# Two mixers, one image pair at a time: the next pair's statistics, logits and softmax among row 7's steps, and row 0's keys and queries in two parts

## Chip, cores and metric

The kernel runs on one core of a Trainium2 chip, in one launch. The metric is device time in microseconds; before the change it is 3754.8 us, the median of three runs (3750.45 to 3756.43). Less is better.

## The reference, cut to what matters

```python
# x: (16, 56, 56, 192) float32
x = x + outlook(_gn(x))     # first mixer
x = x + windows(_gn(x))     # second mixer
# _gn: 32 groups of 6 channels, mean and variance over all positions of an image
# outlook: a = softmax over 9 of (x @ W_attn + b_attn) per head (6 heads); v = x @ W_v + b_v
#          y = sum over the 3x3 neighbourhood of a * v;  y @ W_proj + b_proj
# windows: roll by (-3, -3), 7x7 windows, qkv = xw @ qkv_weight.T + qkv_bias, 12 heads of 16
#          softmax(q*k/4 + relative bias + shift mask) @ v, @ proj_weight.T + proj_bias, roll back
```

## The kernel before, in words

Two images are worked on together (a pair; 192 channels of two images fill three tiles of 128 partitions: tile 0, tile 1 with half of each image, tile 2). A hardware loop runs over the eight pairs. The activation `xa` of a pair stays in SBUF. Within one pass:

1. **Outlook.** Seven chunks of 8 rows each. TensorE repeats attention weights over channels (`reps`, L480), VectorE multiplies them with shifted values (L1339), GpSimd and accumulating DMAs add the nine products, TensorE projects. The logits and softmax of a chunk are worked out during the chunk before it. For chunk 0 that is done at the end of the pass before.
2. **Statistics of the second norm.** VectorE's `bn_stats` and `bn_aggr`, small vector steps (`moments`, L1386), one-column and two-column matmuls that average over groups (`group_moments`, L568), a square root on ScalarE, then `xw`, the normalized row 0.
3. **Windows.** Eight rows of eight windows, each row 392 tokens. Row w+1's queries, keys and values are made while row w's attention runs. A row has eight steps; a step handles two windows and half of the heads: scores (L671) on TensorE, bias and maximum (L1436, L1439, L1446) on VectorE, subtraction (L1667) on GpSimd, exponential (L1055) on ScalarE, sum and reciprocal (L1453, L1456) on VectorE, product (L1674) on GpSimd, transpose of the probabilities (`turn_probs`, L700) on TensorE, copy to SBUF (L1065) on ScalarE, and for every second step the product with the values (`attend`, L717). Scores run three steps ahead of `turn_probs`. The values go from PSUM to `vs` (L1049) and from there by four DMAs per half row, on SP's queue (L290), to `vbd`, which `attend` reads.
4. **Row 7 and the end of the pass.** In row 7 no further row has to be prepared. There stand the last loads of the next pair (`turn_next`), the output transposes of rows 5 and 6 (`turn_out`, L735), the group means and variances of the next pair (`group_means`, `group_variances`, steps 4 and 5), its square root (an `ACT_TABLE_LOAD` for Sqrt in step 5, one for Exp in step 6) and its normalized chunk 0 (`normalize`, step 6). After row 7 come, one behind another: the logits of chunk 0 (L380 to L384), the wide part of its values, the output projection of row 7, `turn_logits`, the softmax on VectorE and ScalarE, its split into three bfloat16 parts (`soft_split`, `back`), row 7's output transposes, and `turn_weights` (L426), on which the next pass's first `reps` wait.

The order on each engine is written out by hand; each engine executes its own list in order and waits on counting semaphores. So a wait holds back all that stands behind it on that engine. PSUM has eight banks; R0, R1 (4, 5), TURN_BANK (6) and Y_BANK (7) are used in turn, banks 0 to 3 hold scores. The steps that the change touches are in `ring`, `ring_last`, `beside` and `window_row`, each of which exists once per engine.

Of the kernel before, what the change touches and what calls it, by code (L numbers as in the profile page):

```python
# [9 lines left out]
ALU = mybir.AluOpType  # L10
ACT = mybir.ActivationFunctionType
# [62 lines left out]
QUERIES = SLOT + N  # L74
ONE = 16
# [9 lines left out]
def mixer(nc, x, wa, ba, wv, bv, wp, bp, wqkv, bqkv, wo, bo, table, sel_in, gmat_in, mask_in, out):  # L85
    ctx = ExitStack()
    with ctx:
# [90 lines left out]
        e_agg = sem("e_agg"); e_kept = sem("e_kept"); g_two = sem("g_two"); xw_zero = sem("xw_zero")  # L178
# [17 lines left out]
        counted = [e_agg, e_kept, g_two, xw_zero, *x_in, x_turned, x_kept, x_stat, g_agg, g_table, g_mean, g_dev, g_sq, g_var, g_std, g_rstd,  # L196
# [130 lines left out]
        def _(pe):  # L327
# [31 lines left out]
            def group_variances(g, bank):  # L359
                pe.wait_ge(g_sq, ONE + g + 1)  # L360
# [99 lines left out]
            middle(5, wot, 0, 2, bias[:, 4, :].unsqueeze(2), 1).then_inc(bout_mm, 1)  # L460
            pe.wait_ge(w_cast, 1)

            def first_weights(G):
                turn_weights(G, 0, FIRST_BANK)
                pe.wait_ge(a_kept, ONE + 2 * G + 1)
                turn_weights(G, 1, FIRST_BANK)

            with pe.Fori(0, NP) as i:
# [42 lines left out]
                def prepare(c, n):  # L511

                    G = G0 + c
                    if n < 2:
                        logits_part(G + 1, n, SOFT_BANK)
# [76 lines left out]
                first_weights(G0)  # L592
                pe.wait_ge(v_kept, ONE + T * (G0 + 1))
                pe.wait_ge(ot_kept, ONE + NT * NW * i)
# [18 lines left out]
                def first_keys(banks):  # L613

                    a, b, src = P[:, banks[0], 0:RT], P[:, banks[1], 0:RT], xw[:, 0, :, :]
# [4 lines left out]
                    mm(a, wt[:, 0, C:C + 128], src[:, 0], start=False, stop=True).then_inc(k_mm, 1)  # L620
                    pe.wait_ge(xw_first, ONE + 2 * i + 2)
                    mm(b, wt[:, 2, C + 64:C + 192], src[:, 2], start=False, stop=True).then_inc(k_mm, 1)

                def queries_wide(w, banks):
                    if w > 0:
                        pe.wait_ge(xw_ok, ONE + T * ((NW - 1) * i + w))
# [31 lines left out]
                def scores(w, s):  # L658
# [3 lines left out]
                    if s == 0:  # L662
                        pe.wait_ge(q_kept, ONE + T * (NW * i + w + 1))
                        pe.wait_ge(k_kept, ONE + T * (NW * i + w + 1))
# [11 lines left out]
                def probs_banks_free(w, s):  # L676
# [3 lines left out]
                    if s % 2 == 1:  # L680
                        pe.wait_ge(y_kept, ONE + PAIRS * R + s // 2)
                    elif w < NW - 1:
                        if s in (2, 4) and w >= 2:
# [6 lines left out]
                    elif s == 6:  # L690
                        pe.wait_ge(ot_kept, ONE + NT * (R - 1) + 2)
# [52 lines left out]
                def beside(w, s):  # L744

                    S = STEPS * (NW * i + w) + s
                    if w < NW - 1:
                        if s in (1, 3) and w >= 2:
# [12 lines left out]
                    elif s == 5:  # L761
                        pe.wait_ge(p_kept, ONE + 2 * S + 1)
                        turn_out(w - 1, 0, Y_BANK)
                        pe.wait_ge(p_kept, ONE + 2 * S + 2)
                        turn_out(w - 1, 1, TURN_BANK)
                    elif s == 7:
                        pe.wait_ge(p_kept, ONE + 2 * S + 1)
                        turn_out(w - 1, 3, Y_BANK)

                def ring(w, s):  # L770
# [3 lines left out]
                    if s == 0:  # L774
                        pe.wait_ge(vs_kept, ONE + 4 * R + (4 if w else 2))
# [18 lines left out]
                    elif s == 4:  # L794
                        pe.wait_ge(k_kept, ONE + T * (R + 1) + 3)
                        if w >= 1:
                            if w >= 2:
                                pe.wait_ge(ot_kept, ONE + NT * (R - 2) + 4)
                            out_wide(w - 1, (R0, R1))
                        else:  # L800
                            window_values(0, 1, (R0, R1))
                    elif s == 5:
                        if w >= 1:
                            pe.wait_ge(fin_ok, ONE + T * (R - 1) + 1)
                            out_middle(w - 1, R0)
                            pe.wait_ge(fin_ok, ONE + T * (R - 1) + 2)
                            turn_next(w, 2, R1)
                    elif s == 6:
                        if w >= 1:
                            pe.wait_ge(fin_ok, ONE + T * R)  # L810
                            pe.wait_ge(x_kept, x_count + 3)
                        else:
                            pe.wait_ge(vs_kept, ONE + 4 * (R + 1))
                        window_values(w + 1, 0, (R0, R1))
                    else:
                        pe.wait_ge(vs_kept, ONE + 4 * (R + 1) + 2)
                        window_values(w + 1, 1, (R0, R1))

                def ring_last(s):
# [947 lines left out]
```

## Time and profile before

| what | value |
|---|---|
| median of three runs | 3754.8 us |
| time of the profiled execution | 3750.84 us |
| its span in the trace | 3749.0 us |
| PE (matmuls) busy | 3429.7 us, 91% |
| PEld (weight loads) busy | 1935.3 us, 52% |
| DVE busy | 2759.6 us, 74% |
| ACT busy | 1912.0 us, 51% |
| POOL busy | 2400.4 us, 64% |
| chain that ended last, by engine | PE 62%, issue 10%, DVE 9%, ACT 8%, DMA 5%, POOL 4% |
| mean granted TensorE clock | 0.956 |

Busy time of PE is an upper bound, since matmuls are pipelined and their ends are modelled. The pass repeats eight times, so a microsecond that is won in each pass is eight in the whole. The granted clock is 1 at 2.4 GHz and 0.5 at 1.2 GHz.

### The profile page before, as it was taken

The page shows a single profiled execution, that of the slowest core. Times are in us where ns is not written, and L with a number is a line of the kernel's source. Part 1 is how long each engine was busy: PE and PEld are TensorE (multiplying, and loading weights), DVE is VectorE, ACT ScalarE, POOL GpSimd, SP SyncE. Part 2 cuts the span into 40 slices and gives each one's busy share as a digit, 9 for nine tenths or more (in the row PEclk, how much of TensorE's full clock was granted, in tenths as well). Part 3 has the DMA queues.
Part 4 walks back from the last instruction along what each step waited for, and adds up shares of the span by engine and source line. Part 5 has one row for each costly group of instructions (what it writes and reads, how often), then busy time and mean ns, then how long its engine had stood idle before and what let it go on. Part 6 is the DMA issues. An engine that isn't in the chain of part 4 may idle for free.

```text
span 3749.0 us, 107677 instructions
## 1 busy us (share of the span) xinstructions
PE 3429.7 (91%) x39700; PEld 1935.3 (52%) x39700; DVE 2759.6 (74%) x4953; ACT 1912.0 (51%) x4042; POOL 2400.4 (64%) x1888
## 2 busy tenths in 40 slices
PE   6989989899898998989989899899998999999998
PEld 3446644466445663356634566345653456534665
DVE  5967769677696776967769677786768767687675
ACT  3446644456435654356643566345554356544565
POOL 2767747677376774767747676466755667566674
PEclk7999989999899998999989999999999999999999
DMA  4722237222371223612246122561215512164221
GB/s 108 141 71 68 72 71 141 64 80 66 81 143 44 82 75 79 135 56 76 69 94 133 52 74 65 101 122 55 80 58 116 106 55 82 55 125 103 61 76 55
DMA packets 204359, 317.64 MB, mean 85 GB/s; under 512 B 16922, under 2 KB 176154, under 8 KB 203802
## 3 DMA queue, kind: packets, MB, share of 16 engines
q0 software_dynamic: 31936, 148.66, 20.3%
q1 hardware_dynamic: 171866, 161.61, 14.7%
q8 instruction: 343, 5.62, 0.6%
q14 instruction: 214, 1.75, 0.1%
HBM read 45.97 MB, written 38.54 MB: 23 GB/s over the span
## 4 chain that ended last, share of the span: by engine, by line
PE 62%; issue 10%; DVE 9%; ACT 8%; DMA 5%; POOL 4%; SPq 1%; ACTq 0%; DVEq 0%; POOLq 0%
PE P L717 5%; PE P L700 5%; PE P L480 5%; PE P L333 4%; PE P L335 4%; PE P L671 4%; PE P L342 3%; PE P L650 3%; DMA prod<-prod 3%; DVE prod L1339 3%; PE P L341 3%; PE P L653 3%; PE P L735 3%; PE P L336 2%; ACT kbd L1038 2%
## 5 line engine op out<-in xcount | busy, mean ns | idle before, releaser
L1667 POOL TENSOR_TENSOR sp__70<-sp__70,mx 128x588 f32<-128x588 f32 x512 | 600.2, 1172 | 639.5 <-DVE mx L1446 638.9
L1339 DVE TENSOR_TENSOR prod<-P,vpad 128x896 f32<-128x896 f32 (+1 forms) x768 | 791.3, 1051 | 111.3 <-PE P L480 100.1
L1674 POOL TENSOR_TENSOR sp__70<-sp__70,rc 128x588 f32<-128x588 f32 x512 | 600.3, 1173 | 13.0 <-DVE rc L1456 13.0
L1436 DVE TENSOR_TENSOR sp__70<-P,relb 128x196 f32<-128x196 f32 x512 | 184.5, 360 | 493.7 <-PE P L671 493.7
L1065 ACT ACTIVATE pt<-P 98x294 f32<-98x294 f32 x1024 | 431.7, 423 | 178.6 <-PE P L700 176.4
L1587 POOL DMA_DIRECT2D prod<-prod x216 | 201.5, 933 | 471.7 <-DVE prod L1339 466.2
L480 PE MATMUL P<-at,sel 108*128 108x448 bf16 x1512 | 427.7, 362 | 34.6 <-DVE prod L1339 31.0
L700 PE MATMUL P<-ident,sp__70 113*98 113x113 f32 x3072 | 395.7, 266 | 23.1 <-ACT pt L1065 13.2
L1446 DVE TENSOR_REDUCE mx<-sp__70 128x12 f32<-128x588 f32 x512 | 389.6, 761 | 9.4
L1055 ACT ACTIVATE sp__70<-sp__70 128x588 f32<-128x588 f32 x512 | 360.9, 705 | 64.9 <-POOL sp__70 L1667 64.2
L700 PEld LDWEIGHTS P<-ident,sp__70 113*98 113x98 f32 x3072 | 329.0, 131 | 117.9 <-issue 56.2
L1453 DVE TENSOR_REDUCE sm<-sp__70 128x12 f32<-128x588 f32 x512 | 387.0, 756 | 0.5
L480 PEld LDWEIGHTS P<-at,sel 108*128 108x128 bf16 x1512 | 112.7, 98 | 404.7 <-issue 205.4
L671 PE MATMUL P<-kbd,qs 32*64 32x98 f32 x12288 | 298.1, 259 | 19.9 <-DVE sp__70 L1439 14.4
L1603 POOL TENSOR_TENSOR psum_p<-psum_p,prod 128x1344 f32<-128x1344 f32 x96 | 298.2, 3106 | 7.1 <-DVE prod L1339 2.9
L1439 DVE TENSOR_TENSOR sp__70<-P,relb 128x392 f32<-128x392 f32 x512 | 284.7, 556 | 0.8
L717 PE MATMUL P<-pt,vbd 98*32 98x49 f32 x12288 | 221.0, 218 | 63.3 <-DMA vbd<-vs 37.9
L1049 ACT ACTIVATE vs<-P 98x192 f32<-98x192 f32 x512 | 127.8, 333 | 281.2 <-PE P L650 281.1
L671 PEld LDWEIGHTS P<-kbd,qs 32*64 32x64 f32 x12288 | 199.4, 130 | 104.9 <-issue 76.5
L1660 POOL TENSOR_SCALAR xr<-xa,bout 128x392 f32<-128x392 f32 x192 | 246.3, 1285 | 0.0
L717 PEld LDWEIGHTS P<-pt,vbd 98*32 98x32 f32 x12288 | 184.9, 114 | 105.1 <-issue 48.5
L1461 DVE COPY yt<-P 128x294 f32<-128x294 f32 x256 | 118.9, 465 | 159.6 <-PE P L717 157.9
(241 smaller groups left out, 7392.9 us busy)
## 6 DMA issues: line engine op xcount, KB each, us to landing
prod<-prod POOLq DMA_DIRECT2D x216, 672.0 KB, 5.5
vbd<-vs SPq DMA_DIRECT2D x512, 147.0 KB
xin<-in_x SPq DMA_DIRECT2D x126, 336.0 KB, 4.0
out<-ot SPq DMA_DIRECT2D x184, 168.0 KB, 2.4
out<-ot SPq DMA_DIRECT2D x80, 84.0 KB
wn<-in_L_conv_qkv_weight SPq DMA_DIRECT2D x2, 432.0 KB, 6.2
wno<-in_L_conv_proj_weight SPq DMA_DIRECT2D x2, 144.0 KB, 6.3
self<-in_sel SPq DMA_DIRECT2D x3, 91.1 KB
```

The lines of the kernel that those rows point to most:

```text
L480: last = mm(P[:, 2 * (n % 2) + b, 0:CT], sel[:, k, :], at[:, col:col + CT], start=True, stop=True)
L671: last = mm(P[half * SLOT:(half + 1) * SLOT, r, part * 2 * N:(part + 1) * 2 * N], qs[rows, w % 2, j, tok:tok + SLOT], kbd[rows, w % 2, j, ...
L700: last = turn(P[0:2 * N, bank, c * QUERIES:(c + 1) * QUERIES], sp_[0:QUERIES, s % SOFTS, g * 2 * N:(g + 1) * 2 * N], ident[0:QUERIES, 0:QU ...
L717: last = mm(P[32 * r:32 * r + 32, Y_BANK, col:col + N], vbd[w % 2][:, 2 * p + half, m, 2 * HD * g:2 * HD * (g + 1)], pt[:, (q + m) % KEPT, ...
L1055: go(sp_[:, s % SOFTS, :], sp_[:, s % SOFTS, :], ACT.Exp).then_inc(p_exp, 1)
L1065: go(pt[:, (STEPS * w + s) % KEPT, 3 * b:3 * b + 3, :, :], src, ACT.Copy).then_inc(p_kept, 1)
L1339: tt(by_row(dst), by_row(P[:, b:b + len(op), 0:CT]), val, ALU.mult).then_inc(prod_ok, 1)
L1446: red(mx[:, b, :], sp_[:, b, :].rearrange("p (h k) -> p h k", h=NH), AX.X, ALU.max).then_inc(t_max, 1)
L1453: red(sm[:, b, :], sp_[:, b, :].rearrange("p (h k) -> p h k", h=NH), AX.X, ALU.add).then_inc(p_sum, 1)
L1603: tt(y0[:] if n == PADD - 1 else psum_p[:], slot(0) if n == 0 else psum_p[:], slot(k), ALU.add).then_inc(padd_ok, 1)
L1667: tt(per_head(sp_[:, b, :]), per_head(sp_[:, b, :]), spread(mx[:, b, :]), ALU.subtract).then_inc(t_sub, 1)
L1674: tt(per_head(sp_[:, b, :]), per_head(sp_[:, b, :]), spread(rc[:, b, :]), ALU.mult).then_inc(p_norm, 1)
```

## The change

It does four things. First, row 0 of the windows: keys and queries are made for the first `EDGE` = 211 tokens, which suffice for steps 0 to 3, and for the other 181 tokens in step 0 (`others`); the second half of row 0's values is made in step 1 and no longer in step 4, and row 1's queries, keys and values move accordingly (`ring_first`). ScalarE loads the Exp table after it has kept the first keys and queries. Second, the moments of tiles 0 and 2 are averaged before tile 1's are there. Third, row 7: `stat_x` and `aggregate` one step earlier; group means in step 2, variances in step 3, both table loads in ScalarE's step 3, `normalize` in step 4, the logits of the next pair's chunk 0 in step 5, `turn_logits` and row 6's first three output transposes in step 6, the softmax's maximum and shift in step 6, its sum and first split in step 7, the wide values in step 7. Fourth, the end of the pass: attention, the middle values, the output projection of row 7, `turn_weights` with two output transposes between its parts, two more behind. The wait for the last output tile (`ot_kept`) goes from the head of a pass to the point before the logits of chunk 1.

```diff
 # TensorE
-                def group_moments():
-                    pe.wait_ge(g_sq, ONE + 2 * i + 2)
+                def group_moments(part):
+                    pe.wait_ge(e_sq, ONE + 2 * i + part + 1)
                     for j in range(T):
-                        last = over_group(j, P[:, SOFT_BANK, 2 * j:2 * j + 2], lambda k: gd[:, k, :])
-                    last.then_inc(g_var, 1)
+                        mine = [g for g in GROUPS[j] if (g[1] == 1) == (part == 1)]
+                        for n, (block, k) in enumerate(mine):
+                            last = mm(P[:, j, 0:2], gm[:, block, :], gd[:, k, :],
+                                      start=(part == 0 and n == 0), stop=(part == 1))
+                    if part == 1:
+                        last.then_inc(g_var, 1)
...
-                stay_warm(10, SOFT_BANK)
-                group_moments()
-                stay_warm(8, 0)
+                stay_warm(4, SOFT_BANK)
+                group_moments(0)
+                stay_warm(4, SOFT_BANK)
+                group_moments(1)
+                stay_warm(8, SOFT_BANK)
...
+                def others(key_bank, banks, query_bank):
+                    R, src = NW * i, xw[:, 0, :, EDGE:RT]
+                    pe.wait_ge(k_kept, ONE + T * R + 1)
+                    middle(key_bank, wt, C, 1, src, RT - EDGE).then_inc(k_mm, 1)
+                    pe.wait_ge(k_kept, ONE + T * R + 2)
+                    pe.wait_ge(p_kept, ONE + 2 * STEPS * R + 1)
+                    first, second = wide(banks, wt, 0, src, RT - EDGE)
...
+                    pe.wait_ge(k_kept, ONE + T * (R + 1))
+                    middle(query_bank, wt, 0, 0, src, RT - EDGE).then_inc(q_mm, 1)
...
+                def ring_first(s):
+                    R = NW * i
+                    if s == 0:
+                        others(R0, (R1, Y_BANK), R0)
+                    elif s == 1:
+                        pe.wait_ge(q_kept, ONE + T * (R + 1))
+                        window_values(0, 1, (R0, R1))
+                    elif s == 2:
+                        pe.wait_ge(vs_kept, ONE + 4 * R + 4)
+                        queries_wide(1, (R0, R1))
...
                     elif s == 2:
                         pe.wait_ge(ot_kept, ONE + NT * (R - 2) + 2)
                         turn_out(w - 2, 3, R0)
+                        pe.wait_ge(ot_kept, ONE + NT * (R - 2) + 3)
+                        group_means(2 * i + 2, R1)
                     elif s == 3:
+                        group_variances(2 * i + 2, R1)
+                    elif s == 4:
                         pe.wait_ge(ot_kept, ONE + NT * (R - 2) + 4)
+                        pe.wait_ge(g_std, ONE + 2 * i + 3)
                         out_wide(w - 1, (R0, R1))
-                    elif s == 4:
+                    elif s == 5:
                         pe.wait_ge(fin_ok, ONE + T * (R - 1) + 1)
                         out_middle(w - 1, R0)
+                        pe.wait_ge(t_add, ONE + 2 * STEPS * NW * (i + 1))
+                        logits(CHUNKS * (i + 1), FIRST_BANK)
+                    elif s == 6:
                         pe.wait_ge(fin_ok, ONE + T * (R - 1) + 2)
-                        group_means(2 * i + 2, R1)
-                    elif s == 5:
-                        group_variances(2 * i + 2, R1)
-                    elif s == 6:
-                        turn_out(w - 1, 2, R0)
+                        turn_out(w - 1, 0, R1)
+                        turn_out(w - 1, 1, R0)
+                        turn_out(w - 1, 2, 1)
+                    elif s == 7:
+                        values_wide(0)
+                        pe.wait_ge(p_kept, ONE + 2 * STEPS * (R + 1))
+                        turn_out(w - 1, 3, TURN_BANK)
...
+                            if w == NW - 1 and s == 6:
+                                turn_logits(CHUNKS * (i + 1), FIRST_BANK)
...
-                first_keys((0, 1))
-                keys_middle(0, 2)
-                queries_wide(0, (R0, R1))
-                queries_middle(0, TURN_BANK)
+                first_keys((0, 1), EDGE)
+                first_queries((R0, R1), TURN_BANK, EDGE)
                 pe.wait_ge(vs_zero, ONE + 3 * i + 3)
-                for s in range(AHEAD):
-                    scores(0, s)
+                scores(0, 0)
+                scores(0, 1)
                 window_values(0, 0, (R0, R1))
+                scores(0, 2)
+                pe.wait_ge(vs_kept, ONE + 4 * NW * i + 2)
+                other_keys((R0, R1))
...
                 attend(w, PAIRS - 1)
-                pe.wait_ge(t_add, ONE + 2 * STEPS * NW * (i + 1))
-                logits(Gn, FIRST_BANK)
-                values_wide(0)
-                pe.wait_ge(g_std, ONE + 2 * i + 3)
+                pe.wait_ge(ot_kept, ONE + NT * (R - 1) + 3)
+                values_middle(0)
                 out_wide(w, (R0, R1))
-                turn_logits(Gn, FIRST_BANK)
-                values_middle(0)
                 pe.wait_ge(fin_ok, ONE + T * R + 1)
                 out_middle(w, R0)
+                turn_weights(Gn, 0, FIRST_BANK)
+                pe.wait_ge(ot_kept, ONE + NT * R)
                 for t, bank in enumerate((R1, TURN_BANK, Y_BANK, R0)):
                     turn_out(w, t, bank)
+                    if t == 1:
+                        pe.wait_ge(a_kept, ONE + 2 * Gn + 1)
+                        turn_weights(Gn, 1, FIRST_BANK)
 # ScalarE, row 7
-                    elif s == 5:
-                        keep_out(w - 1, 0, Y_BANK)
-                        keep_out(w - 1, 1, TURN_BANK)
+                    elif s == 3:
                         load_table(4 * i + 4, ACT.Sqrt)
                         deviation(2 * i + 2, R1)
-                    elif s == 6:
-                        keep_out(w - 1, 2, R0)
+                        load_table(4 * i + 5, ACT.Exp)
+                    elif s == 4:
                         act.wait_ge(g_ready, ONE + 2 * i + 3)
                         act.wait_ge(y_mm, ONE + STEPS * (NW * i + w))
-                        normalize(CHUNKS * (i + 1), 0)
-                        load_table(4 * i + 5, ACT.Exp)
+                        normalize(Gn, 0)
+                    elif s == 5:
+                        keep_logits(Gn, FIRST_BANK)
+                    elif s == 6:
+                        keep_out(w - 1, 0, R1)
+                        exps(Gn, FIRST_BANK)
+                        keep_out(w - 1, 1, R0)
+                        keep_out(w - 1, 2, 1)
                     elif s == 7:
-                        keep_out(w - 1, 3, Y_BANK)
+                        back(Gn, 0, FIRST_BANK)
+                        act.wait_ge(border_ok, ONE + i + 2)
+                        keep_values(Gn, 0, 0, ORDER[0], 0)
+                        keep_values(Gn, 0, 1, ORDER[1], 0)
 # GpSimd: row 2's stage_norm in row 0's steps 3 to 5 (was 5 and 6), clear_border in row 7's step 5 (was 6)
```

## Rows read from the trace of the kernel before

**Rows 1.** Busy time by stretch (`x` instructions), second pass: PE, PEld, DVE, ACT, POOL, clock.
```profile
933.00:989.50 56.50, 43.59 (x551) 27.47 (x551) 26.49 (x61) 28.74 (x59) 16.96 (x16) 0.81 0.18 53
1158.40:1194.20 35.80, 29.74 (x461) 20.00 (x460) 21.07 (x42) 18.13 (x45) 19.26 (x19) 0.89 0.13 40
1194.20:1225.40 31.20, 30.71 (x520) 19.75 (x518) 24.45 (x50) 18.67 (x45) 24.22 (x23) 1.00 0.21 62
1225.40:1393.00 167.60, 159.85 (x2651) 104.70 (x2650) 124.93 (x255) 100.91 (x240) 120.89 (x109) 1.00 0.24 73
```

**Rows 2.** The instructions of line 1023: count, ns min/median/max, first and last start.
```profile
L1023 ACT ACTIVATE xw<-xa,gb,ga x8: 735/736/737, 222.0 to 3441.1; 128x392 f32<-128x392 f32 x8
```

**Rows 3.** TensorE's timeline (start, us, [idle <-releaser]), end of a pass.
```profile
946.16 0.74 PE L700 MATMUL P<-ident,sp__70 113*98 113x113 f32 x6
...
959.30 1.37 PE L700 MATMUL P<-ident,sp__70 113*98 113x113 f32 x6
963.95 0.89 PE L735 MATMUL P<-ident,fin 128*112 128x128 f32 x3 [3.28 <-ACT pt L1065]
...
987.00 0.99 PE L426 MATMUL P<-identb,comb 112*108 112x112 bf16 x8 [4.27 <-DVE comb L1249]
...
989.50 0.95 PE L480 MATMUL P<-at,sel 108*128 108x448 bf16 x2
```

**Rows 4.** Busy time by stretch, around the lower clock (columns as in Rows 1).
```profile
951.30:954.70 3.40, 2.72 (x25) 2.37 (x25) 3.17 (x10) 2.13 (x5) 1.79 (x2) 1.00 0.01 2
954.80:971.80 17.00, 13.07 (x134) 7.47 (x133) 1.18 (x4) 8.20 (x15) 1.91 (x3) 0.50 0.14 38
...
1115.20:1118.50 3.30, 3.30 (x8) 1.55 (x7) 2.83 (x4) 0.00 (x0) 3.12 (x2) 0.50 0.95 182
...
1152.80:1159.60 6.80, 6.57 (x46) 4.77 (x46) 4.30 (x9) 2.84 (x8) 5.29 (x5) 0.50 0.00 1
...
1183.40:1190.20 6.80, 4.78 (x62) 3.54 (x63) 2.04 (x4) 0.00 (x0) 2.25 (x3) 0.50 0.06 19
```

**Rows 5.** ScalarE's timeline, the two table loads of row 7.
```profile
954.76 1.28 ACT L901 ACT_TABLE_LOAD   x1
...
956.35 0.26 ACT L905 ACTIVATE gstd<-P,eps_s 128x3 f32<-128x3 f32 x1
...
962.10 1.28 ACT L901 ACT_TABLE_LOAD   x1
```

**Rows 6.** The page's groups: busy, mean ns of one, for one step of a window row.
```profile
L1667 POOL TENSOR_TENSOR sp__70<-sp__70,mx 128x588 f32<-128x588 f32 x512 | 600.2, 1172 | 639.5 <-DVE mx L1446 638.9
...
L1446 DVE TENSOR_REDUCE mx<-sp__70 128x12 f32<-128x588 f32 x512 | 389.6, 761 | 9.4
L1055 ACT ACTIVATE sp__70<-sp__70 128x588 f32<-128x588 f32 x512 | 360.9, 705 | 64.9 <-POOL sp__70 L1667 64.2
```

**Rows 7.** TensorE's timeline, moments to the end of row 0.
```profile
1137.87 1.72 PE L350 MATMUL P<-gd,gm 128*128 128x2 f32 x14
1139.45 1.89 PE L367 MATMUL P<-sel,identb 108*128 108x512 bf16 x8
1141.63 0.59 PE L617 MATMUL P<-xw,wt 64*128 64x392 f32 x1 [0.29 <-DVE xw L1425]
...
1150.07 0.58 PE L671 MATMUL P<-kbd,qs 32*64 32x98 f32 x24 [0.69 <-ACT qs L1031]
...
1158.36 1.33 PE L700 MATMUL P<-ident,sp__70 113*98 113x113 f32 x6
...
1185.42 1.23 PE L717 MATMUL P<-pt,vbd 98*32 98x49 f32 x48 [4.67 <-DMA vbd<-vs]
...
1194.22 0.75 PE L700 MATMUL P<-ident,sp__70 113*98 113x113 f32 x6
```

**Rows 8.** SP's timeline, the values' second half of row 0 sent to `vbd`.
```profile
1178.17 3.26 SPq L290 DMA_DIRECT2D vbd<-vs  x4
```

**Rows 9.** ScalarE's timeline, the last instruction of the kernel.
```profile
3748.21 0.54 ACT L945 ACTIVATE at<-P 108x448 bf16<-108x448 bf16 x1 [0.71 <-PE P L426]
```

More of the change, by code:

```diff
@@ L74 @@
 QUERIES = SLOT + N
+EDGE = 3 * N + SLOT
 ONE = 16
@@ L661, in scores @@
                     pe.wait_ge(t_add, ONE + 2 * S)
-                    if s == 0:
+                    if w == 0 and s == 0:
+                        pe.wait_ge(qh_kept, ONE + T * (i + 1))
+                        pe.wait_ge(kh_kept, ONE + T * (i + 1))
+                    elif s == (4 if w == 0 else 0):
                         pe.wait_ge(q_kept, ONE + T * (NW * i + w + 1))
@@ L747, in beside @@
                     if w < NW - 1:
-                        if s in (1, 3) and w >= 2:
+                        if s == 3 and w == 0:
+                            pe.wait_ge(p_kept, ONE + 2 * S + 1)
+                            queries_middle(1, Y_BANK)
+                        elif s in (1, 3) and w >= 2:
                             pe.wait_ge(p_kept, ONE + 2 * S + 1)
@@ L1108, in ring, with ring_first @@
                             keep_window_values(w + 1, 1, m, (R0, R1)[m])
+                def ring_first(s):
+                    if s == 0:
+                        keep_keys(0, 2, R0, EDGE)
+                        keep_queries(0, 0, R1, EDGE)
+                        keep_queries(0, 1, Y_BANK, EDGE)
+                        keep_queries(0, 2, R0, EDGE)
+                    elif s == 1:
+                        for m in range(2):
+                            keep_window_values(0, 1, m, (R0, R1)[m])
+                    elif s == 2:
+                        keep_queries(1, 0, R0)
+                        keep_queries(1, 1, R1)
+                    elif s == 3:
+                        keep_queries(1, 2, Y_BANK)
+                        keep_keys(1, 0, R0)
+                        keep_keys(1, 1, R1)
+                    elif s == 4:
+                        keep_keys(1, 2, R0)
+                    elif s < 7:
+                        for m in range(2):
+                            keep_window_values(1, s - 5, m, (R0, R1)[m])
                 def ring_last(s):
-                    w = NW - 1
+                    w, Gn = NW - 1, CHUNKS * (i + 1)
                     if s == 0:
@@ L1147, in window_row @@
                             ring_last(s)
[L1149 to L1154 removed]
+                for n in range(T):
+                    keep_first_keys(n, n)
+                for n, bank in enumerate((R0, R1, TURN_BANK)):
+                    keep_first_queries(n, bank)
+                load_table(4 * i + 3, ACT.Exp)
                 exp_step(0, 0)
[L1156 removed]
                 act.wait_ge(vs_zero, ONE + 3 * i + 2)
@@ L1518, in window_row @@
                         extras(w, s)
-                for s in range(AHEAD):
+                for s in range(2):
                     score_bias(0, s)
                     score_max(0, s)
-                for s in range(AHEAD - 1):
-                    prob_sum(0, s)
+                prob_sum(0, 0)
+                score_bias(0, 2)
+                score_max(0, 2)
+                prob_sum(0, 1)
                 for w in range(NW):
@@ L1711, in _ @@
                     stage_residual(0, j)
-                for s in range(AHEAD):
+                for s in range(2):
                     shift_step(0, s)
                 normalize_step(0, 0)
+                shift_step(0, 2)
                 for w in range(NW):
```

229 lines of the change are left out of this document (121 added, 108 removed).

## The prediction

> **What bounds the kernel now.** I read the page's shares first: TensorE is busy 91% of the span, VectorE 74%, GpSimd 64%. Then I cut one pass into stretches by busy time [rows 1]. Rows 1 to 7 of the windows are bound by TensorE: row 1 takes 31.20 us, of which it is busy 30.71, and rows 2 to 6 are busy 159.85 of 167.60 us. The change leaves these alone. Two stretches are not like them. From the start of row 7 to the next pass's first `reps`, 933.0 to 989.5, there are 56.5 us with 43.59 busy at a mean clock of 0.81; row 0 takes 35.8 us with 29.74 busy at 0.89 [rows 1]. A pass takes (3441.1 - 222.0) / 7 = 459.9 us [rows 2], so these two are a fifth of it.
>
> TensorE's timeline shows what ends the waits there. In row 7 it stands 3.28 us before an output transpose, at 963.95, for a copy of the probabilities on ScalarE, and 4.27 us before `turn_weights`, at 987.00, for the last softmax split on VectorE [rows 3]: logits, softmax, split and copies run one behind another with only some projections beside them. ScalarE loads its tables there, 1.28 us each [rows 5]. In row 0 TensorE stands 4.67 us at 1185.42 for the DMAs that bring the second half of the values to `vbd` [rows 7]; they were issued from 1178.17 on [rows 8], because those values are made only in step 4.
>
> The clock comes on top. From 954.8 to 971.8, 17.0 us, the granted clock is 0.50 (1.2 GHz), with 13.07 us of busy TensorE in it. Before it fell, TensorE was busy 2.72 of 3.40 us, much of it on one-column matmuls for the means. It is low again for 6.8 us twice, at 1152.8 and at 1183.4 (during the DMA wait), and for 3.3 us at 1115.2 behind other one-column matmuls [rows 4].
>
> **Part by part.** All times are of the second pass, and a gain counts eight times.
>
> *End of the pass.* The change takes no matmul out. Work at full clock: 43.59 busy, less half of the 13.07 that ran at the low clock [rows 1, 4], is 37.1 us. This is the floor for a stretch that TensorE fills. I then laid out the new order on the four engines with durations from the timeline, starting at 933.0. Steps 0 and 1 keep their two waits for the probabilities, 1.0 us. The group means run in step 2 from 942.4, VectorE's deviations end at 945.45, the variances run 945.55 to 947.2. ScalarE now holds both table loads before step 4's copy of the probabilities; by the rows a load and its first activation are 1.28 us and about 0.3 us [rows 5], so behind the square root the Exp load keeps ScalarE until 949.3, and `attend` in step 4 waits from 948.4 to 949.65: 1.25 us. Behind this `attend` on TensorE stands everything else, so this wait counts in full. `normalize` ends at 952.6, before TensorE comes to the logits at 955.0, which hide it. Maximum, shift, exponential, sum and first split then run on VectorE and ScalarE from 958.1 to 962.1, beside steps 6 and 7 (transposes, 2.5 us of wide values). The second and third splits end at 966.6, while TensorE is in the middle values and row 7's projection until 969.8: the 4.27 us wait before `turn_weights` goes, and the projection itself is what is late next. The output transposes wait some 0.9 us for row 7's last sum, and half of them stand before the second `turn_weights`, 0.75 us, hiding the copy of the first. The rest are short hand-overs, 0.7 us. Waits: 1.0 + 1.25 + 0.9 + 0.7 = 3.9 us. Path: 37.1 + 3.9 = 41.0 us.
>
> For the clock I take 5 us of busy work at 1.2 GHz instead of 13, 2.5 us, since the one-column matmuls are now 1.7 and 1.7 us between dense work, as at 1115.2, where only 3.3 us were low [rows 4]. Sum: 43.5 us against 56.5, **a gain of 13.0 us**. Bounds: no low clock, 41.0 us, gain 15.5; the low clock as long as before (+6.5) and twice the waits, 51.5 us, gain 5.0.
>
> The Trainium skill (ScalarE: Activation LUTs, section What ACT_TABLE_LOAD costs) adds to each load of another set a drain of about 1.38 us. This case's trace disagrees: from the load at 954.76 to the square root's start at 956.35 are 1.59 us, load and first activation included [rows 5]. By the rule the two loads, now back to back before step 4, would cost 2.76 us more a pass.
>
> Edits with one answer: `clear_border` in step 5 stands on GpSimd between the products of steps 6 and 7, some 1 us, and the sum of step 7 comes later than that, so nothing. `stat_x` one step earlier makes VectorE's step-2 bias 0.6 us late, inside the hand-over sum. The wait for the last output tile moves behind the first `reps`; that tile is copied at about the time TensorE gets there, 0, and up to 1 us if the copy is late, as VectorE's first product stands behind `reps` only and the second behind the wait. The output stores keep their order on SP; each slot of `ot` is written some 8 us or more after its last store was issued, so they hold nobody.
>
> *Moments, keys and queries.* Of the 14 matmul instructions from 1137.87 to 1139.45 [rows 7] eight go ahead of tile 1's statistics, so 0.9 us leave the path; the four warming matmuls before the rest make it start 0.3 us later. Gain 0.6 us. From the first key matmul at 1141.63 to the first score at 1150.07 are 8.4 us [rows 7]. With 211 of 392 columns the matmuls, 7.75 us, take 4.2, and the last query copy 0.5: 4.7, gain 3.7. The Exp load leaves ScalarE's path to the keys and lies beside the first scores and their maximum. Together **4.3 us**; from 3.3 (short matmuls limited by their weight loads) to 4.9.
>
> From the first score to `turn_probs` of step 0 are 8.3 us [rows 7], a chain of one step over four engines: three reads of 0.7 to 0.8 on VectorE, 0.70 on ScalarE, two of 1.17 on GpSimd [rows 6]. The new order puts the values after the second score and the other keys behind them: about 6.7 us at full clock, 9.3 at half. The clock was low here before [rows 4] and TensorE again waits between scores, so I take 8.3 unchanged, from -1.0 to +1.6.
>
> *Row 0.* Work at full clock: 29.74 less half of 4.78 [rows 1, 4] is 27.35. `others` adds 2.95 (181 columns three times, with weight loads). The 4.67 us wait goes: the second half's values are now copied at 1161, their DMAs landed 7.3 us after the first issue (1178.17 to 1185.42) [rows 7, 8], so at 1168.5, and `attend` needs them at about 1178. The first half, copied at 1151, lands at 1158.4, needed at 1161.4. New waits are in `others`, which shares R0, R1 and Y_BANK with copies of ScalarE, and in the last step, where TensorE has 1.2 us of work: 1.4 us. 27.35 + 2.95 + 1.4 = 31.7 against 35.8, **gain 4.1 us**; from 0.1 (low clock 2.4, waits 3) to 5.5. GpSimd's `stage_norm` in steps 3 to 5, 0.7 us each, fits in its gaps: it is busy 19.26 of 35.8 us [rows 1].
>
> *Sum.* A pass gains 13.0 + 4.3 + 4.1 = 21.4 us; eight make 171.2. In the last pass nothing follows, and the kernel ended with ScalarE's copy at 3748.21 [rows 9], 0.2 us after where `reps` would begin; it will end with the copy and the store of the last output tile, some 2.7 us after it. 171.2 - 2.7 = 168.5. The profiled execution took 3750.84, 1.84 more than its span and 4.0 less than the median: 3582.3 by it, 3586.3 by the median. I predict **3584**. Own range: passes from 8.4 to 26.9 us give 3538 to 3686.
>
> **Rivals.** What a measurement of this kernel can tell from no change is 0.2%, 7.5 us.
>
> 1. *The end of the pass gives only its lower bound, 5.0 us.* The low clock lasts as long as before, and ScalarE's list, now with tables, `normalize`, logits and copies between the probabilities, is late at each. For it: a low stretch of 17.0 us behind means and variances [rows 4]. Against: after it TensorE had long waits [rows 3], which now are filled. (5.0 + 8.4) x 8 - 2.7 = 104.5: 3650.
> 2. *Row 0 gives nothing but the moments' 0.6 us.* The halves return in step 0 as a chain: key copy, query matmul, query copy, three times through the same banks. For it: ScalarE is in each link. Against: it is busy 18.13 of 35.8 us [rows 1]. (13.0 + 0.6) x 8 - 2.7 = 106: 3648.
> 3. *Each table load holds ScalarE 1.3 us longer when it stands before work that is due.* The two would move the wait in step 4 from 1.25 to 3.9: 2.6 x 8 = 21, 3605. Against: the load at 954.76 [rows 5]. This is the skill's rule above.
> 4. *Slower: the clock falls behind the means in row 7 and stays at 1.2 GHz to the end of the stretch, and again from the first scores through row 0.* Price: of the 37.1 us, 24.6 come after step 3, so +24.6; in and before row 0 some 35 us, so +35; less 8 for waits that it fills: 52 against a gain of 21.4, 31 a pass, 4000. It decides from 21.4 us of full-clock work a pass that is done at half clock on top. For it: the longest low stretch today held 13 us [rows 4]. Against: dense work ended each of them.
>
> **How the numbers follow.** Forecast 0.62; rival 1 0.17; rival 2 0.09; rival 3 0.04; rival 4 0.04; 1 and 2 together 0.04 (5.6 x 8 - 2.7 = 42, 3710; half of it so near to nothing that I count it as same). The range, 3545 to 3660, holds rivals 1 to 3 and most of the forecast's own. Faster by over 0.2%: 0.62 + 0.17 + 0.09 + 0.04 + 0.02 = 0.94; within 0.2%: 0.02; slower: 0.04.
>
> **What would show it.** The distance between two `xw` (L1023) should be 438.5 us instead of 459.9. Row 7 to `reps`: 43.5; the wait for comb (L1249) before `turn_weights` gone; TensorE waiting about 1.2 us in step 4 for pt (L1065). First key matmul to first score 4.7; row 0 31.7 long with no wait for vbd. Rows 1 to 6 unchanged at 31.2 and 33.5 each; if they grow, something moved collides there, and this would make the prediction wrong. So would a granted clock of 0.5 for more than 10 us after the means.

## The result, and the profile after

The changed kernel takes **3623.88 us**, the median of 4 runs (3622.52 to 3625.28), against 3752.62 us of the kernel before in the same comparison: a ratio of 0.9656, 95% interval 0.9639 to 0.9673. It is 128.7 us faster. The prediction said 3584, a gain of 168.5; the time lies inside its range, and a quarter of the gain is missing. The profiled execution took 3622.52 us, its span is 3620.7.

First the page's shares and its group of waits, then one pass cut at the same places as in [rows 1]: row 7 to `reps`, row 0, row 1, rows 2 to 6, and the stretch from the first score to row 0. The columns are those of [rows 1].

```profile
PE 3391.4 (94%) x39908; PEld 1934.4 (53%) x39908; DVE 2774.4 (77%) x4977; ACT 1918.9 (53%) x4114; POOL 2401.7 (66%) x1888
...
PE 65%; issue 11%; ACT 8%; DVE 8%; POOL 4%; DMA 3%; ACTq 1%; DVEq 0%; SPq 0%; POOLq 0%
```

```profile
909.99:956.85 46.86, 41.34 (x551) 27.05 (x551) 28.21 (x61) 28.63 (x60) 16.96 (x16) 0.89 0.20 62
677.41:710.73 33.32, 30.51 (x483) 20.12 (x481) 20.75 (x44) 21.39 (x54) 20.45 (x19) 1.00 0.17 54
710.73:741.97 31.24, 30.75 (x518) 19.78 (x519) 25.64 (x53) 18.02 (x41) 24.90 (x23) 1.00 0.17 51
741.97:909.99 168.02, 160.19 (x2652) 104.79 (x2650) 125.40 (x257) 101.13 (x242) 121.31 (x110) 1.00 0.24 73
670.89:677.41 6.52, 5.37 (x96) 3.82 (x97) 5.39 (x11) 3.77 (x9) 4.61 (x4) 1.00 0.01 4
```

Rows 1 to 6 are as they were. TensorE's busy share went from 91% to 94%, and its busy time fell by 38 us; 173 us of the kernel ran at 1.2 GHz instead of 332. Cutting all passes at the same instructions and taking the mean over the first seven gives this table:

| stretch of a pass, us | before | after | gain | predicted gain |
|---|---|---|---|---|
| row 7 to the next `reps` | 55.44 | 46.64 | 8.80 | 13.0 |
| `reps` to `xw` (the moments) | 152.61 | 152.03 | 0.58 | 0.6 |
| first key matmul to first score | 8.44 | 5.32 | 3.12 | 3.7 |
| first score to row 0 | 7.94 | 6.74 | 1.20 | 0 |
| row 0 | 35.61 | 33.32 | 2.29 | 4.1 |
| rows 1 to 6 | 199.31 | 199.26 | 0.05 | 0 |
| pass | 459.88 | 443.84 | 16.04 | 21.4 |

The distance between two `xw` is (3327.8 - 220.9) / 7 = 443.84 us; the row answers to [rows 2]:

```profile
L1085 ACT ACTIVATE xw<-xa,gb,ga x8: 734/737/739, 220.9 to 3327.8; 128x392 f32<-128x392 f32 x8
```

Seven distances give 112.3 us, the head 1.1, and the last pass, after which nothing follows, 15.0: together 128.3, the difference of the spans (3749.0 - 3620.7, but for rounding).

TensorE's timeline of the end of the second pass answers to [rows 3] (start, us, [idle <- releaser]):

```profile
919.39 1.62 PE L353 MATMUL P<-mv,gm 128*128 128x1 f32 x14
...
923.13 2.71 PE L353 MATMUL P<-gsq,gm 128*128 128x1 f32 x14 [0.98 <-DVE gsq L1301]
...
928.01 1.23 PE L754 MATMUL P<-pt,vbd 98*32 98x49 f32 x48
...
951.19 0.62 PE L429 MATMUL P<-identb,comb 112*108 112x112 bf16 x8
...
952.90 0.41 PE L429 MATMUL P<-identb,comb 112*108 112x112 bf16 x4
953.15 0.82 PE L772 MATMUL P<-ident,fin 128*112 128x128 f32 x6
956.85 0.55 PE L481 MATMUL P<-at,sel 108*128 108x448 bf16 x2 [2.87 <-issue]
```

The 4.27 us wait for `comb` is gone: `turn_weights` follows the projection without a wait. The last output transposes end at 953.97, 43.98 us after row 7 began. Then TensorE stands 2.87 us before `reps` for nothing that the profile shows. At that place ends the body of its hardware loop. That the instructions behind the jump back come late is a reading of this row; the experiments test it. Before the change the pass's first instructions were `turn_weights`, and they waited for `comb` anyway. The list of all waits, longest in total first, has the same for all passes (us in total, times, longest):

```profile
PE P L772 <- ACT pt L1137: 43.9, 48, 1.0
...
PE P L481 <- issue: 22.0, 7, 3.5
```

The low clock in row 7 has changed its shape. In this stretch TensorE is busy throughout:

```profile
923.60:933.80 10.20, 10.11 (x100) 6.88 (x100) 6.13 (x13) 5.75 (x11) 5.43 (x6) 0.50 0.01 2
```

The granted clock falls 3.9 to 5.2 us after the first of the one-column means, as before (4.1 to 5.8), in every pass: for 10.2 us in six of eight and 6.8 us in two, where it was 13.7 or 17.1 us. It falls a second time at the change of pass. Behind the 2.87 us pause the first `reps` run at 1.2 GHz, for 3.4 us in six of the seven changes and 6.8 us in one:

```profile
957.77:961.18 3.41, 3.41 (x11) 0.44 (x8) 1.84 (x2) 0.00 (x0) 0.00 (x0) 0.50 0.02 4
```

TensorE's timeline of keys, scores and row 0 answers to [rows 7]:

```profile
665.57 0.44 PE L625 MATMUL P<-xw,wt 64*128 64x211 f32 x1 [0.29 <-DVE xw L1529]
...
670.89 0.58 PE L706 MATMUL P<-kbd,qs 32*64 32x98 f32 x24 [0.58 <-issue]
...
697.26 0.82 PE L754 MATMUL P<-pt,vbd 98*32 98x49 f32 x48 [1.03 <-ACT pt L1137]
...
701.19 0.58 PE L706 MATMUL P<-kbd,qs 32*64 32x98 f32 x24 [0.72 <-ACT kbd L1111]
...
710.73 0.47 PE L737 MATMUL P<-ident,sp__70 113*98 113x113 f32 x3 [0.95 <-ACT pt L1137]
```

The wait for `vbd` (4.67 us) is gone, three waits for ScalarE's copies stand in its place, 2.7 us together.

Last, ScalarE's timeline of the two table loads answers to [rows 5]:

```profile
922.97 1.28 ACT L963 ACT_TABLE_LOAD   x1
924.27 0.20 ACT L963 ACTIVATE table_t<-eps_s 128x1 f32<-128x1 f32 x1
925.87 0.26 ACT L967 ACTIVATE gstd<-P,eps_s 128x3 f32<-128x3 f32 x1 [1.40 <-PE P L353]
926.15 1.28 ACT L963 ACT_TABLE_LOAD   x1
927.45 0.20 ACT L963 ACTIVATE table_t<-eps_s 128x1 f32<-128x1 f32 x1
927.56 0.40 ACT L1137 ACTIVATE pt<-P 98x294 f32<-98x294 f32 x1
```

A useful copy starts 1.41 us after the second load began. The Trainium skill (ScalarE: Activation LUTs, section What ACT_TABLE_LOAD costs) adds a drain of about 1.38 us to each switch of tables. By an estimate from that figure the copy would start at 928.8 or later; the trace has it at 927.56.

### The profile page after: what moved, and what is told of

Its sections match the earlier page's. It is cut to its first block, busy times and chain, and to the rows that moved or that the text cites. A ratio compares the mean times of both kernels' runs of the same rounds, so it can differ in the third digit from the quotient of the medians.

```text
span 3620.7 us, 108243 instructions
## 1 busy us (share of the span) xinstructions
PE 3391.4 (94%) x39908; PEld 1934.4 (53%) x39908; DVE 2774.4 (77%) x4977; ACT 1918.9 (53%) x4114; POOL 2401.7 (66%) x1888
## 4 chain that ended last, share of the span: by engine, by line
PE 65%; issue 11%; ACT 8%; DVE 8%; POOL 4%; DMA 3%; ACTq 1%; DVEq 0%; SPq 0%; POOLq 0%
PE P L737 5%; PE P L754 5%; PE P L481 5%; PE P L338 5%; PE P L336 5%; PE P L345 4%; PE P L706 4%; PE P L344 4%; PE P L682 3%; DVE prod L1435 3%; DMA prod<-prod 3%; PE P L685 2%; PE P L339 2%; ACT kbd L1110 2%; PE P L772 2%
## 5 line engine op out<-in xcount | busy, mean ns | idle before, releaser
L706 PE MATMUL P<-kbd,qs 32*64 32x98 f32 x12288 | 299.7, 260 | 17.1 <-DVE sp__70 L1543 6.6
L1046 ACT ACTIVATE xa<-P,bias 128x448 f32<-128x448 f32 x168 | 107.3, 639 | 257.0 <-PE P L499 217.9
L1713 POOL TENSOR_TENSOR psum_p<-prod 128x1344 f32<-128x1344 f32 x56 | 171.8, 3069 | 80.7 <-DMA prod<-prod 80.7
```

The costliest lines, as they stand in the source:

```text
L706: last = mm(P[half * SLOT:(half + 1) * SLOT, r, part * 2 * N:(part + 1) * 2 * N], qs[rows, w % 2, j, tok:tok + SLOT], kbd[rows, w % 2, j, ...
L1713: tt(y0[:] if n == PADD - 1 else psum_p[:], slot(0) if n == 0 else psum_p[:], slot(k), ALU.add).then_inc(padd_ok, 1)
```

## The experiments

Each ratio is against the kernel before, run on the same chip in the same comparison. The changed kernel was not run again in these comparisons; its 3623.88 us are those of the first one. The median of the kernel before moved between 3752.6 and 3756.0 us from one comparison to the next, so a difference to the changed kernel is known to some 4 us only.

### The jump back: three kernels

**a_edge2**: TensorE's loop takes four rounds of two passes. **a_edge8**: its eight passes are written out. **b_edge2**: the first edit on the kernel before.

```diff
-            with pe.Fori(0, NP) as i:
+            with pe.Fori(0, NP // 2) as i_pe:        # a_edge2, b_edge2
+             for u_pe in range(2):
+                i = 2 * i_pe + u_pe
+            for i in range(NP):                      # a_edge8
```

> The changed kernel, with TensorE's loop over the passes written as four rounds of two passes each; nothing else differs, the other engines keep their eight rounds. Theory A: the 2.9 us that TensorE stands without a releaser between the last output transpose of a pass and the first reps of the next are the price of the loop's jump back. Four of the seven such waits (22.0 us in all) then go: 12 to 13 us faster than the changed kernel, about 3611 us, and the wait stays in three passes. Theory B: TensorE waits there for a copy or for VectorE, which the profile does not name: no difference, 3624 us.

> The changed kernel, with TensorE's eight passes written out, without a loop on that engine. Theory A (the jump back costs 2.9 to 3.5 us): all seven waits go, 22 us faster than the changed kernel, about 3602 us. Theory B: no difference, 3624 us. A third outcome, slower, would mean that fetching straight code cannot keep up with TensorE.

> The kernel before, with TensorE's loop as four rounds of two passes. Theory A says that here the jump back lies inside the 4.27 us in which TensorE waits for the last softmax split before turn_weights, at the head of the pass: no difference, 3753 us. If the jump cost something of its own here too, it would be 12 us faster, 3740 us.

Measured: a_edge2 3608.05 us (3606.32 to 3613.63), ratio 0.9610 (0.9594 to 0.9626), 15.8 us faster than the changed kernel. a_edge8 3598.21 us (3595.03 to 3601.17), ratio 0.9578 (0.9562 to 0.9594), 25.7 us faster. b_edge2 3756.1 us, ratio 1.0001 (0.9992 to 1.0011): no difference. The waits of a_edge2 show three jumps that are left of seven:

```profile
PE P L483 <- issue: 10.7, 3, 3.6
```

In a_edge8 `reps` stands right behind the last transposes:

```profile
953.12 0.83 PE L772 MATMUL P<-ident,fin 128*112 128x128 f32 x6
953.78 0.54 PE L481 MATMUL P<-at,sel 108*128 108x448 bf16 x2
```

Row 7 to `reps` is 43.8 us in each of its first seven passes, where the prediction had 43.5. So the pause at the jump takes about 3.1 us a pass (22.0 / 7), 25.7 us came from writing the passes out, and the pause costs something only where no other wait covers it: in the kernel before, the nine waits for `comb` (39.6 us) did, and are still 39.6 us in b_edge2. What is gained beyond the 22.0 us fits the clock: in a_edge8 it does not fall at the first `reps` in any pass, and `reps` to `xw` takes 151.2 us instead of 152.0. What in the jump takes the time is not shown.

### The two halves, each alone

**front_only** is the kernel before with the moments, the split of row 0's keys and queries and `ring_first`; **end_only** is it with the new row 7 and end of the pass. The diffs are the corresponding parts of the change.

> The kernel before with the front of the change alone: moments in two parts, first half of row 0's keys and queries ahead, the other half in step 0, values in step 1; row 7 and the end of the pass stay as they were. Theory A (the two halves of the change add up): the stages of the changed kernel are its own here too, 0.6 us less before the keys, first key to first score 5.3, first score to probabilities 6.5, row 0 33.3, so 0.6 + 3.1 + 1.3 + 2.3 = 7.3 us a pass less, 58 in all, 3695; row 7 to reps stays 55 to 56. Rival: what is won ahead of row 0 is given back at the waits of the old end (the last softmax split before turn_weights), and less than 40 us come, over 3712.

> The kernel before with the end of the pass alone: next pair's statistics, logits and softmax beside row 7; keys and row 0 stay as they were. Theory A: row 7 to reps 46.6 us instead of 55.4, 8.8 us a pass, 70 less 2.7 at the very end, 3685; key to score 8.4 and row 0 35.6 with its wait for the values. Together with the front alone the sum of gains is 125 to 130, that of the whole change (128.7). Rival: the moved Exp table load or the loop's jump costs more or less with the old front, and the sum is off by over 10 us.

Measured: front_only 3703.08 us, ratio 0.9858 (0.9843 to 0.9873), 52.9 us less than the kernel before; end_only 3681.18 us, ratio 0.9799 (0.9784 to 0.9814), 74.8 us less. The sum is 127.8, the whole change gave 128.7: the halves add up, within the 5 to 6 us that each interval leaves. Both came out some us off the stage sums (58 and 67). With the old end, the front makes the stretch from row 7 to `reps` 56.2 us instead of 55.4. The end's 74.8 us are 8 more than its stages gave; its trace, of the slowest of its four runs, is 65.0 us shorter than that of the kernel before.

### Row 0: values early without the split, and the split alone

**b_vals** is the kernel before with only the second half of row 0's values in step 0, and row 1's queries and keys one step later. **a_unsplit** is the changed kernel with that row 0 instead of its own.

```diff
 # ring(w, s), TensorE, step 0
-                        pe.wait_ge(vs_kept, ONE + 4 * R + (4 if w else 2))
-                        queries_wide(w + 1, (R0, R1))
+                        if w == 0:
+                            pe.wait_ge(vs_kept, ONE + 4 * R + 2)
+                            window_values(0, 1, (R0, R1))
+                        else:
+                            pe.wait_ge(vs_kept, ONE + 4 * R + 4)
+                            queries_wide(w + 1, (R0, R1))
```

> The kernel before, with one part of the change alone: in row 0 the second half of the values is made in step 0 instead of step 4, and row 1's queries and keys move one step back; keys and queries of row 0 stay whole. Theory A: the 4.67 us wait for the DMAs to vbd goes and with it the low clock that follows it (6.8 us with 4.85 busy, worth 2.4): row 0 from 35.6 to some 29.5 us, 8 x 6 = 48 us faster, 3705 us. Theory B: the wait turns into others in row 0, as it did in the changed kernel (33.3 us with the second halves of keys and queries in it, some 30.4 without them): 8 x 5.2 = 42, so if row 0 comes out above 31 us the split was not what kept the changed kernel's row 0 at 33.3.

> The changed kernel with row 0's keys and queries whole ahead of the first score again, its second-half values in step 0, row 1's queries and keys a step later; new end of the pass and moments ahead stay. It tells what the split itself brings. By the stages of the runs so far: first key to first score 8.4 instead of 5.3, first score to probabilities 8.0 instead of 6.5, row 0 30.0 instead of 33.3: 1.3 us a pass more, 3634 against 3624. Rival B (the split is a net cost, since its matmuls of 181 columns pay their weight loads again in row 0): faster than the changed kernel, under 3616.

Measured: b_vals 3719.65 us, ratio 0.9901 (0.9885 to 0.9918), 34.5 us faster. Row 0 in its second pass:

```profile
695.42:724.89 29.47, 27.11 (x460) 18.26 (x461) 20.89 (x43) 17.69 (x44) 19.42 (x19) 1.00 0.16 49
```

Over its first seven passes row 0 takes 29.8 us on average, 5.8 less than before, without a wait for `vbd`. Eight times that would be 46, near the 48 of theory A; 34.5 came. Row 7 to `reps` (56.3 instead of 55.4) and `reps` to `xw` (153.6 instead of 152.6) are each 1 us longer, though nothing was changed in them. From row 7 to the end of the low clock behind the first `reps`, 23.9 us of each pass are at 1.2 GHz instead of 22.4 on average, and between there and `xw` 27 us in the seven passes together instead of 14. That explains a part; the rest is open. The kernel before is not the same in each execution either: in b_edge2, whose time did not change, `reps` to `xw` is 153.6 us too. a_unsplit takes 3633.82 us (3629.34 to 3637.2), ratio 0.9675 (0.9661 to 0.9688): 9.9 us slower than the changed kernel, as expected, though the intervals of the two ratios overlap a little (0.9661 to 0.9688 and 0.9639 to 0.9673). So most of what row 0 gives comes from the earlier values. By the stages the split brings 3.1 us before the first score and 1.0 behind it, and costs 3.7 in row 0 (29.6 in a_unsplit). Nearly all of this cost is work: TensorE is busy for 30.51 us of row 0 in the changed kernel, for 27.11 in b_vals, 3.4 less. That leaves 0.4 us a pass. With the last pass, whose row 0 takes 31.07 us in a_unsplit, the stages of the split make some 5 us of the 9.4 between the two spans. The rest lies in stretches that the two kernels share, and what puts it there is open.

### Row 0: the order of ScalarE's copies

```diff
 # ScalarE, row 0
                         keep_queries(1, 2, Y_BANK)
                         keep_keys(1, 0, R0)
-                        keep_keys(1, 1, R1)
 ...
                         keep_probs(w, s, 0)
+                        if w == 0 and s == 4:
+                            keep_keys(1, 1, R1)
```

> The changed kernel with one copy of ScalarE moved in row 0: the second key copy (kbd, R1) stands behind the first copy of the probabilities of step 4 instead of ahead of it. In the changed kernel TensorE stands 1.03 us there for pt and 0.72 us a step later for kbd. Theory A (the waits of row 0 are the order of ScalarE's copies): the first wait goes, the second grows by at most the 0.4 us that the copy comes later, row 0 32.7 us instead of 33.3, 4 to 8 us in all, 3616 to 3620. Rival B (the chain over GpSimd and VectorE is the limit and pt only shows it): row 0 stays 33.3 and the time within 0.1% of the changed kernel's.

Measured: **a_swap** 3613.78 us (3611.9 to 3615.33), ratio 0.9621 (0.9608 to 0.9634), 10.1 us faster than the changed kernel. Row 0 is 32.23 us in all eight passes, 1.09 less. Theory A holds: the first wait went with the move of one copy. My size for it was too small. In its timeline `attend` of step 4 follows without a wait:

```profile
697.52 0.58 PE L706 MATMUL P<-kbd,qs 32*64 32x98 f32 x24
698.03 0.82 PE L754 MATMUL P<-pt,vbd 98*32 98x49 f32 x48
...
701.96 0.58 PE L706 MATMUL P<-kbd,qs 32*64 32x98 f32 x24 [0.72 <-ACT kbd L1111]
```

The wait for `kbd` didn't grow: it hangs on the last key copy, not on the moved one.

### The clock behind the means

**a_cols64** takes the matmuls of the group means, of the variances and of the means that the second norm uses as a first estimate over 64 equal columns instead of one. **a_cols64_edge8** has TensorE's passes written out as well.

```diff
-                    last = over_group(j, P[:, bank, j:j + 1], lambda k: mv[:, k, 0:1])
+                    last = over_group(j, P[:, bank, j * WC:(j + 1) * WC],
+                                      lambda k: mv[:, k, 0:1].to_broadcast([128, WC]))   # WC = 64
```

> The changed kernel with the group means, variances and the estimate's means as matmuls over 64 equal columns instead of one (same weights, a repeated operand; more columns, nothing left out). Theory A (one-column matmuls, mostly weight loads, are what goes ahead of the low clock in row 7): the 10.2 us at 0.5 that follow the means of step 2 shrink or go, up to 5 us a pass less the 0.3 to 0.8 that the wider columns cost, 3585 to 3605. Rival B (something else in that stretch, a short wait or the transposes, lets the clock fall): low time stays at 170 us in all and the kernel takes 3624 to 3632.

> The same, with TensorE's eight passes written out instead of a loop. If the clock and the jump back are separate costs, the gain over the changed kernel is that of the wide columns alone plus the 25.7 us measured for writing out: 3560 to 3580 under theory A, 3598 to 3606 under rival B. If the low clock was a part of what the jump cost (a pause at the edge), the two gains overlap and the sum is smaller by up to 10 us.

Measured: a_cols64 3603.02 us (3596.65 to 3607.21), ratio 0.9588 (0.9575 to 0.9602), 20.9 us faster than the changed kernel. a_cols64_edge8 3574.91 us (3572.38 to 3582.15), ratio 0.9521 (0.9508 to 0.9534): 49.0 us faster, where the two edits alone gave 46.6. They add up. The means of the second pass in a_cols64, and the stretch that in the changed kernel was low:

```profile
917.90 1.67 PE L354 MATMUL P<-mv,gm 128*128 128x64 f32 x14
```

```profile
922.20:932.40 10.20, 9.12 (x117) 5.22 (x116) 8.17 (x18) 6.96 (x14) 6.58 (x7) 1.00 0.01 3
```

The 14 matmuls take 1.67 us instead of 1.62, so the 63 more columns are nearly free. Just before the place where the clock falls in the changed kernel, TensorE does as much by the records in both kernels; the first row is the changed kernel's, the second that of a_cols64:

```profile
920.20:923.60 3.40, 2.42 (x43) 2.08 (x42) 3.30 (x9) 2.04 (x4) 2.30 (x2) 1.00 0.08 25
```

```profile
918.80:922.20 3.40, 2.43 (x42) 2.08 (x42) 3.30 (x9) 2.12 (x4) 2.30 (x2) 1.00 0.08 25
```

Behind the means the clock stays up in six of eight passes; in two it is low for 6.8 us. 98 us of the kernel are at 1.2 GHz instead of 173. In a_cols64_edge8 it stays up in three passes. Two of its stretches from row 7 to `reps`, the first with 6.8 us at the low clock, the second with none:

```profile
908.01:950.23 42.22, 39.42 (x550) 26.00 (x551) 27.68 (x61) 27.55 (x58) 16.98 (x16) 0.92 0.18 56
1346.02:1386.23 40.21, 36.49 (x550) 24.15 (x551) 27.59 (x61) 27.55 (x58) 16.99 (x16) 1.00 0.19 59
```

So the stretch takes 40.2 us without a low clock, 42.2 with 6.8 us of it, 43.8 to 43.9 with 10.2: 10.2 us at 1.2 GHz cost 3.6 us a pass. Why the clock still falls in some passes with 64 columns is open.

### The best version

> Everything found that helps, together: the changed kernel with the moved key copy, the 64-column means and variances and TensorE's passes written out. 3574.9 without the moved copy; with it 3567 to 3571 if the theory of a_swap holds, 3575 if not.

**a_best** (moved copy, 64 columns, passes written out) takes 3572.31 us (3568.81 to 3575.36), ratio 0.9515 (0.9502 to 0.9528): the fastest here, 51.6 us below the changed kernel. Row 0 is 32.37 us instead of a_cols64_edge8's 33.48, but the runs of the two overlap; that the moved copy gives its 9 us on top is not shown. Behind the means the clock falls for 6.8 us in six of its eight passes, so the wide columns do not keep it up for certain.

## Why the prediction was right and where it was wrong

**End of the pass: 13.0 predicted, 8.8 measured.** This step failed, by a term that wasn't in it. Its mechanism held: the wait for `comb` went, and without the jump the stretch is 43.8 us against 43.5. The waits named in it are there. In the second pass of a_cols64, with no low clock, they are 1.0 us in steps 0 and 1 (as predicted), 1.08 in step 4 (1.25) and 0.4 for row 7's last sum (0.9); 0.97 us before the variances stood only among the hand-overs (0.7 together). But "the projection itself is what is late next" was not the whole answer. Removing the wait for `comb` uncovered TensorE's jump back, 3.1 us a pass: the row was there to be asked about, since in [rows 3] the wait stands on the first instructions behind the loop's head. It is 22.0 us by the list of waits, and 25.7 with all that went in a_edge8, of the 39.8 that are missing.

That 43.5 came so near to 43.8 is luck: its parts were each off by about a microsecond and cancelled. *The clock* was mis-sized: 2.5 us taken, 3.6 measured. I had set the short low stretch at 1115.2 [rows 4] as the model, and it lasted 10.2 us, with all of it busy. By the prediction's own mark, over 10 us at 0.5 behind the means, this step was wrong. *Work and waits* were 41.0 predicted, 40.2 measured (a_cols64_edge8, the stretch without a low clock): 36.5 us of work instead of 37.1, 3.7 of waits instead of 3.9. The work was too high because I halved only the busy time of the first low stretch. Before the change the clock was low a second time, just ahead of `reps`:

```profile
985.60:989.50 3.90, 1.40 (x13) 1.24 (x13) 0.61 (x1) 1.62 (x3) 0.00 (x0) 0.50 0.10 30
```

With half of this 1.40 taken off too, the work is 36.4 us. The wait in step 4 for the probabilities doesn't show in the changed kernel's row above, where TensorE, at half speed, comes later itself.

*The baseline* was one pass taken for eight. The second pass of before has 56.5 us here [rows 1]; the mean over seven is 55.4. That alone is 1.06 us a pass, 8.5 in all.

**Moments, keys and queries: 4.3 predicted, 3.7 measured.** The moments gave 0.58 of 0.6. First key to first score took 5.32 instead of 4.7: 0.58 us of it is a wait before the first score that the sum didn't have.

**First score to row 0: no gain predicted, 1.2 measured.** I set a low clock against the shorter list and took the two as equal. In seven of eight passes the clock stays at 2.4 GHz here, and the stretch takes 6.53 us, near the 6.7 that stood in the text for full clock; in the one pass where it falls, 8.0.

**Row 0: 4.1 predicted, 2.3 measured.** Work was nearly right in sum: 27.35 + 2.95 = 30.3 against 30.51 busy at full clock, and the values landed in time. Of the work, the other halves took 3.4 us instead of 2.95 (30.51 less the 27.11 of b_vals). The waits were mis-sized: 2.7 us instead of 1.4. The missing one is `attend` of step 4 behind ScalarE's key copies (a_swap). A microsecond that TensorE loses here counts in full.

**The rivals.** The time lies nearer to rivals 1 and 2 (3650 and 3648) than to 3584; that neither happened is seen in the stages alone. The end gave 8.8 and not 5.0, the front and row 0 gave 7.2 and not 0.6, though each rival held a grain: low clock, chain of copies. Rival 3 fell with ScalarE's rows above. Rival 4 did not happen: behind the means the clock was low for 10.2 us at most, and in row 0 never. The prediction's own range was drawn too tight at its slow end: its 8.4 us a pass leave out the 1.6 us that it allowed for the first score; with them it is 6.8 us, near 3699. Rows 1 to 6 unchanged, 31.24 and 33.55 (rows 2 to 5): right; row 6 takes 33.8 in both kernels.

In sum, per pass: jump 3.1, baseline 1.3 (end 1.1, row 0 0.2), keys 0.6, row 0 1.6, less 1.2 that the scores gave: 5.4, which is 21.4 - 16.0. Seven passes make 37.5, and the last one is 3.7 short: the kernel ends 4.7 us behind its last `turn_weights`, where I had put 2.7. The part before the first `xw` gave 1.1 back, which is less than it varies by: it takes 220.9 to 224.2 us in the traces of the changed kernel and those made from it. That makes 40.1 by the spans.

## What to carry to other kernels

Before a wait at the head of a loop's body is removed, ask what it covers: the jump back stands behind it, and it becomes visible the moment the wait is gone; here the clock fell behind it as well. Where work is moved into a dense stretch, write down for each engine what stands *ahead* of the copy that TensorE waits for; one copy out of order cost 1.1 us a pass here. And take the mean over the passes as the baseline, not the one pass that was read closely.

## What the runs showed of the hardware

- The jump back of TensorE's loop leaves it idle for 2.8 to 3.6 us when nothing covers it (changed kernel, a_edge2), and behind the pause the granted clock was 0.5 for 3.4 or 6.8 us in each of seven changes of pass. With the eight passes written out (a_edge8) there is neither; rows 2 to 5 take 33.52 us against 33.55, row 0 takes 33.48 against 33.32.
- One-column matmuls count as busy in the records, and yet the granted clock went to 1.2 GHz behind them in each of eight passes, once with TensorE busy for 10.11 of the next 10.20 us. With 64 columns in the same time it did so in two of eight (a_cols64), five of eight (a_cols64_edge8) and six of eight passes (a_best). That the columns matter is shown, that they are all that matters is not.
- A table load takes 1.28 us, and a copy of ScalarE started 1.41 us after the load had begun (changed kernel, 926.15 to 927.56); no drain stands between them.
